# An order of work changed: VectorE's taps in the block ahead, and one block's expert layer behind the last scores

## What is computed

```python
def tok(x):                                     # 4 images, c = 64
    y = relu(bn(einsum('oc,bchw->bohw', conv1_w, x) + conv1_b))          # 16 channels
    wdyn = einsum('ok,bkhw->bohw', conv2_w, y) + conv2_b                 # 9 taps a pixel
    return einsum('bckhw,bkhw->bchw', unfold3x3(x), wdyn).reshape(b, h * w, c)

def attn(x):                                    # 4096 tokens of 64
    Q, K, V = x @ Wq + bq, x @ Wk + bk, x @ Wv + bv
    return softmax(Q @ K.T / 8) @ V

def ffn(x):                                     # 32 experts, hidden 16
    idx = argmax(x @ router_w.T + router_b)
    return relu(relu(x @ W1[idx] + b1[idx]) @ W2[idx] + b2[idx])

h = tok(x)
h = h + attn(layernorm(h))
h = h + ffn(layernorm(h))
```

## Time and profile before

| | before |
|---|---|
| median of 3 runs | 1206.12 us (1203.44 to 1207.32) |
| the profiled execution | 1203.22 us |
| its span | 1201.3 us |
| instructions | 29556 |
| idle of VectorE ahead of the copy of z (L1037) | 80.4 us in 16 |
| HBM read and written | 41.77 MB, 4.75 MB |

### The profile page before, as it was taken

How to read it: one execution, slowest core, us unless ns; L and a number is a source line. 1 busy time by engine, 2 the same in 40 slices (tenths; PEclk the granted TensorE clock), 3 DMA queues, 4 the chain that set the end, 5 groups by cost and what they waited for, 6 DMA issues and landing times.

```text
span 1201.3 us, 29556 instructions
## 1 busy us (share of the span) xinstructions
PE 1115.2 (93%) x12890; PEld 481.3 (40%) x12890; DVE 490.8 (41%) x1102; ACT 626.6 (52%) x681; POOL 10.4 (1%) x34
## 2 busy tenths in 40 slices
PE   5878999998999999999999999999899999999974
PEld 1323644443454434343444434444344343434332
DVE  6781774518072451806336081542703030311223
ACT  1545555554656455564555556465555646455531
POOL 3000000000000000000000000000000000000000
PEclk9989999999999999999999999999999999999996
DMA  7344331203032120302112030120000000000000
GB/s 195 82 106 91 83 80 37 57 1 89 1 73 57 36 55 2 91 2 63 28 28 65 1 89 2 38 54 19 19 2 11 2 10 2 10 2 10 2 10 10
DMA packets 11892, 48.52 MB, mean 40 GB/s; under 512 B 2462, under 2 KB 2590, under 8 KB 11372
## 3 DMA queue, kind: packets, MB, share of 16 engines
q1 hardware_dynamic: 11756, 46.53, 16.4%
HBM read 41.77 MB, written 4.75 MB: 39 GB/s over the span
## 4 chain that ended last, share of the span: by engine, by line
PE 65%; DVE 23%; DVEq 5%; issue 4%; DMA 2%; ACT 1%; SPq 0%; ACTq 0%
PE z_ps L592 25%; PE scores L582 23%; DVE hres L896 5%; DVEq L821 5%; PE both L550 4%; PE both L565 4%; DVE tap_product L891 2%; PE both L445 2%; DVE tap_product L846 1%; DVE tap_product L844 1%; DVE stat L842 1%; DVE stat L848 1%; DMA filter_ring<-filters 1%; PE both L546 1%; PE both L513 1%
## 5 line engine op out<-in xcount | busy, mean ns | idle before, releaser
L751 ACT ACTIVATE probs<-scores 128x1024 f32<-128x1024 f32 x480 | 465.4, 1021 | 449.2 <-PE scores L582 449.2
L582 PE MATMUL scores<-g_t,keys_t 64*64 64x512 f32 x4096 | 508.2, 591 | 4.8 <-issue 3.3
L592 PE MATMUL z_ps<-probs,keys 64*64 64x512 f32 x4096 | 510.4, 594 | 0.0
L582 PEld LDWEIGHTS scores<-g_t,keys_t 64*64 64x64 f32 x4096 | 183.8, 134 | 270.2 <-issue 257.8
L592 PEld LDWEIGHTS z_ps<-probs,keys 64*64 64x64 f32 x4096 | 173.4, 134 | 217.0 <-issue 187.6
L972 DVE COPY o_sb<-both 128x512 f32<-128x512 f32 x15 | 10.4, 692 | 459.9 <-PE both L565 459.9
L896 DVE TENSOR_TENSOR hres<-hres,tap_product 128x504 f32<-128x504 f32 (+1 forms) x128 | 89.2, 697 | 10.8 <-issue 0.4
L891 DVE SCALAR_TENSOR_TENSOR tap_product<-filter_ring,w,xin 128x504 f32<-128x504 f32 (+1 forms) x120 | 89.0, 742 | 7.0 <-DMA filter_ring<-filters 3.1
L550 PE MATMUL both<-y_t,w 64*64 64x512 f32 x496 | 66.6, 597 | 0.0
L744 ACT ACTIVATE hidden<-both 128x1024 f32<-128x1024 f32 (+1 forms) x62 | 62.6, 1010 | 3.0 <-PE both L550 3.0
L565 PE MATMUL both<-hidden,w 64*64 64x512 f32 x480 | 60.6, 591 | 0.0
(11 more groups left out here) (129 smaller groups left out, 533.1 us busy)
## 6 DMA issues: line engine op xcount, KB each, us to landing
filter_ring<-filters SPq DMA_DIRECT2D x90, 384.0 KB, 5.2
out_dram<-out_sb SPq DMA_DIRECT2D x32, 128.0 KB, 2.4
xin<-x_dram SPq DMA_DIRECT2D x6, 528.0 KB, 7.3
hidden<-once_dram SPq DMA_DIRECT2D x1, 930.0 KB, 13.1
hidden<-once_dram SPq DMA_DIRECT2D x1, 576.0 KB, 4.9
filters<-filters_sb SPq DMA_DIRECT2D x30, 18.0 KB
xin<-x_dram SPq DMA_DIRECT2D x1, 384.0 KB, 6.4
xin<-x_dram SPq DMA_DIRECT2D x1, 368.0 KB, 7.6
```

The source lines that it names most:

```text
L582: last = T.matmul(scores[rows_of(h), c, r * 512:(r + 1) * 512], keys_t[rows_of(r), n // NQ % 2, g * 128 + 64 * h:g * 128 + 64 * h + 64], g ...
L592: last = T.matmul(z_ps[rows_of(c), h, :], keys[rows_of(h), n // NQ % 2, 2 * g + r, :], probs[rows_of(h), (2 * g + c) % RING, r * 512:(r + ...
L751: A.activation(probs[:, unit % RING, :], scores[:, c, :], ACT.Exp, scale=SCALE if n else first_scale[:, 0:1]).then_inc(probs_ready, 1)
```

## The change

The plan is written anew, and four things follow from it.

- Usual blocks (3 to 15): `fin@n-2` goes from group 2 to 1, `pz` from 3 to 2, `yt` and `lg` from 6 and 7 to 5 and 6. `sum2` of block n+4 stays in group 4, and `sum0 sum1` of block n+5 stand in group 10, behind `ot`. `cc` and `cv` of a pair go from groups 1 and 4 to 4 and 7. Blocks 1 and 2 (`early_groups`) lead over to it.
- Opening: `cc@3` and `cv@3` go from block 0 into the opening, between its power steps.
- The end: `hid0` to `hid3` and `o2` of block 14 go from block 15 into the tail, between `pz@15` and `yt@15`, in the score banks and z's bank; `fin@14` goes behind `lg@15`. Of both last `o2`, ScalarE copies the lower half and VectorE adds the upper (semaphore `lower_copied`).
- SP: the filters of pair 3 are stored before block 1's are spread; a block's spread runs one block further ahead and stands behind the store of the results.

```diff
--- before.py
+++ after.py
@@ -64,7 +64,10 @@
 
 
 NONE = ("sum", "pow", "aw")
-USUAL, FIRST_TAP, TAP_PLACES, LAST = 0, 1, 6, {"hid1": 7, "hid2": 8, "o2": 9}
+USUAL, FIRST_TAP, TAP_PLACES = 0, 1, 6
+
+AT_THE_END = {f"{name}@{BLOCKS - 2}": k for name, k in (("hid0", 7), ("hid1", 8), ("hid2", 7), ("hid3", 8), ("o2", 9))}
+AT_THE_END |= {f"{name}@{BLOCKS - 1}": k for name, k in (("hid1", 7), ("hid2", 8), ("o2", 9))}
 PLACES = 10
 CHUNK = 3
 CHUNKS = TAPS // CHUNK
@@ -79,11 +82,9 @@
 def opening_groups():
     first = "tap0 tap1 tap2 tap3 tap4 tap5"
     return {
-        -1: [*at(0, "c1 " + first), *at(1, "cc cv"),
-             *at(0, "tap6 tap7 tap8 pow0 aw pow1 pow2 pow3 pow4 pow5 xt g")],
+        -1: [*at(0, "c1 " + first), *at(1, "cc cv"), *at(0, "tap6 tap7 tap8 pow0 aw pow1 pow2"), *at(3, "cc"),
+             *at(0, "pow3 pow4 pow5"), *at(3, "cv"), *at(0, "xt g")],
         0: at(1, "sum0 sum1 sum2"),
-        1: at(3, "cc"),
-        2: at(3, "cv"),
         3: at(1, "xt"),
         4: [*at(1, "g"), *at(2, "sum0 sum1 sum2")],
         7: at(2, "xt"),
@@ -94,37 +95,45 @@
     }
 
 
-def behind(m):
-
-    return {2: at(m - 1, "fin"), 3: at(m, "pz"), 6: at(m, "yt"), 7: at(m, "lg"), 10: at(m, "ot"),
-            11: at(m, "hid0"), 12: at(m, "hid1"), 13: at(m, "hid2"), 14: at(m, "hid3"), 15: at(m, "o2")}
-
-
 def merged(*plans):
     return {g: [f for p in plans for f in p.get(g, [])] for g in range(-1, PAIRS + 1)}
 
 
-def second_groups():
-    i, j = NQ, NQ + 1
-    return merged({0: at(i, "sum0"), 1: at(j, "cv"), 2: at(i, "sum1"), 4: at(i, "sum2")}, behind(0),
-                  {8: [*at(i, "xt"), *at(j, "sum0 sum1")], 9: at(i, "g"), 12: at(j, "sum2"), 16: at(j, "xt")})
+def early_groups(n):
+
+    m, i, j = n - 1, 2 * n + 2, 2 * n + 3
+    usual = {2: at(m, "pz"), 3: at(i, "sum0 sum1"), 5: at(m, "yt"), 6: at(m, "lg"), 7: at(i, "sum2"), 8: at(m, "ot"),
+             9: at(m, "hid0"), 10: at(m, "hid1"), 11: at(i, "xt"), 12: at(i, "g"), 13: at(m, "hid2"),
+             14: at(m, "hid3"), 15: at(m, "o2")}
+    if n == 1:
+        return merged(usual, {3: at(j, "cv"), 12: at(j, "sum0 sum1 sum2"), 16: at(j, "xt")})
+    return merged({0: at(i - 1, "g"), 1: at(m - 1, "fin")}, usual,
+                  {4: at(j, "cc"), 7: at(j, "cv"), 12: at(j, "sum0 sum1")})
 
 
 def usual_groups(n):
-    i, j = n + NQ, n + NQ + 1
-    ahead = {1: at(j, "cc"), 4: at(j, "cv")} if j in PAIRED else {}
-    return merged({0: at(NQ + 1, "g")} if n == 2 else {}, ahead,
-                  {0: at(i, "sum0"), 2: at(i, "sum1"), 4: at(i, "sum2")}, behind(n - 1),
-                  {8: at(i, "xt"), 9: at(i, "g")})
+
+    m, i, j = n - 1, n + NQ, n + NQ + 1
+    pair = {4: at(j, "cc"), 7: at(j, "cv")} if j in PAIRED else {}
+    groups = merged({1: at(m - 1, "fin"), 2: at(m, "pz"), 4: at(i, "sum2"), 5: at(m, "yt"), 6: at(m, "lg")}, pair,
+                    {8: at(i, "xt"), 9: at(i, "g"), 10: [*at(m, "ot"), *at(j, "sum0 sum1")]})
+    if n < BLOCKS - 1:
+        return merged(groups, {11: at(m, "hid0"), 12: at(m, "hid1"), 13: at(m, "hid2"), 14: at(m, "hid3"),
+                               15: at(m, "o2")})
+    return groups
 
 
 def last_groups():
+
     m = BLOCKS - 1
-    return merged(behind(m), {16: at(m, "fin")})
+    return merged({2: at(m, "pz"), 3: at(m - 1, "hid0 hid1 hid2 hid3 o2"), 5: at(m, "yt"), 6: at(m, "lg"),
+                   7: at(m - 1, "fin"), 8: at(m, "ot"), 9: at(m, "hid0 hid1 hid2 hid3"), 15: at(m, "o2"),
+                   16: at(m, "fin")})
 
 
 def whole_plan():
-    return [opening_groups(), second_groups(), *(usual_groups(n) for n in range(2, BLOCKS)), last_groups()]
+    return [opening_groups(), early_groups(1), early_groups(2), *(usual_groups(n) for n in range(3, BLOCKS)),
+            last_groups()]
 
 
 def split(fill):
@@ -146,9 +155,7 @@
                         continue
                     name, i = split(fill)
                     k = FIRST_TAP + int(name[3:]) % TAP_PLACES if name.startswith("tap") else USUAL
-                    if i == BLOCKS - 1:
-
-                        k = LAST.get(name, USUAL)
+                    k = AT_THE_END.get(fill, k)
                     count[k] += 1
                     self.of[fill], self.nth[fill], self.earlier[fill] = k, count[k], held.get(k)
                     held[k] = fill
@@ -253,6 +260,7 @@
         filters_loaded = [sem(f"filters_loaded{k}") for k in range(SLOTS)]
         filters_used = [sem(f"filters_used{k}") for k in range(SLOTS)]
         xn_ready, upper_hidden = sem("xn_ready"), sem("upper_hidden")
+        lower_copied = sem("lower_copied")
         y_ready, onehot_ready = sem("y_ready"), sem("onehot_ready")
         out_stored = [sem("out_stored0"), sem("out_stored1")]
         centred_ready, power_written, power_read = sem("centred_ready"), sem("power_written"), sem("power_read")
@@ -332,25 +340,25 @@
             load_image(1, 0, TILES + 2, x_loaded[1])
             sp.dma_start(staged[:, rest_of_it:], once[:, rest_of_it:]).then_inc(once_rest_loaded, 16)
             store_filters(1)
-            spread_filters(1)
             store_filters(3)
-            spread_filters(2)
-            spread_filters(3)
+            for i in range(1, NQ):
+                spread_filters(i)
             for n in range(1, BLOCKS + 2):
                 if n % NQ == 1 and n // NQ + 2 < B:
 
                     sp.wait_ge(xn_ready, NQ * (n // NQ + 1))
                     load_image(n // NQ + 2, 0, TILES + 2, x_loaded[n // NQ % 2])
+                if n > 1:
+                    store_block(n - 2)
                 if n == 1:
                     spread_filters(NQ)
                     store_filters(NQ + 1)
                     spread_filters(NQ + 1)
-                elif n + NQ < BLOCKS:
-                    spread_filters(n + NQ)
-                if n > 1:
-                    store_block(n - 2)
+                    spread_filters(NQ + 2)
+                elif n + NQ + 1 < BLOCKS:
                     if n + NQ + 1 in PAIRED:
                         store_filters(n + NQ + 1)
+                    spread_filters(n + NQ + 1)
             for k in range(2):
                 sp.wait_ge(out_stored[k], 32 * BLOCKS // 2)
 
@@ -707,6 +715,10 @@
                 elif name == "aw":
                     act.wait_ge(a_written, 1)
                     A.copy(a_w[:, :], z_ps[:, 1, 0:128]).then_inc(a_ready, 1)
+                if name == "o2" and i >= BLOCKS - 2:
+                    k = places.of[full]
+                    act.wait_ge(filled[k], places.nth[full])
+                    A.copy(o2_sb[:, :], place[k][:, 0, :]).then_inc(lower_copied, 1)
                 if name.startswith(NONE) or not name.startswith(MINE):
                     return
                 k = places.of[full]
@@ -969,8 +981,11 @@
                     normalise(h2[:, i % 2, :, :])
                     write_normalised(y_block).then_inc(y_ready, 1)
                 elif name == "o2":
-                    V.tensor_copy(o2_sb[:, :], mine[:, 0, :])
-                    settle()
+                    if i < BLOCKS - 2:
+                        V.tensor_copy(o2_sb[:, :], mine[:, 0, :])
+                        settle()
+                    else:
+                        dve.wait_ge(lower_copied, i - (BLOCKS - 3))
                     V.tensor_tensor(o2_sb[:, :], o2_sb[:, :], mine[:, 1, :], ALU.add).then_inc(done, 1)
                 else:
                     if i > 1:
```

## The result

The changed kernel takes 1159.43 us (median of 4 runs, 1157.84 to 1160.31). The ratio to the kernel before is 0.962, 95% interval 0.9597 to 0.9644: 45 us less. The forecast was 1158.5, the range 1151 to 1171.

A forecast was written before the change was run, and what follows sets the result against it. TensorE, busy 93%, was taken as the bound, stalling for late VectorE work. Stalls and gaps 38.2 + expert layer 8.3 + tail 0.8 - opening 1.5 = 45.8 us off 1203.2 or 1206.1 gave 1158.5, range 1151 to 1171.

The forecast's parts named there:

- Fin first, taps later: Blocks' new order: TensorE's stalls at `xt` and `pz` go, worth 19.7 and 12.8 us.
- the 0.18 us added to each stall: At `xt` and `pz`: a stall costs 0.18 us more than its idle figure, which counts from a modelled end.
- The taps' filters: Even blocks: the six taps wait some 6 us for filters and end near 48 us; cost nothing.
- Block 1: Block 1, with its own order: layer norm ends about 3 us before `xt`, the stall goes; 2.1 us shorter.
- The gap at the block's head: Before a block's first value group: a 0.41 us wait for z's copy goes in 14 blocks, 5.7 us.
- the spacing forecast for the blocks: Blocks 3, 5, 7, 9, 11 about 66.4 us apart, those with a pair about 68.1, before 70.6 to 71.0.
- Expert layer and tail: Block 14's expert layer: 8.3 us off block 15, 0 added behind `pz`; rest of tail 0.8 less.
- the 0.7 and 0.1 less and the 0.85 more: Tail: `pz` not waiting for `fin` 0.7 less, ScalarE copying half of `o2` 0.1 less, `ot` waiting for `fin` 0.85 more.
- 2.4 us between cold and warm: Tail from `ot` through the hidden fills: a warm clock gives 2.4 us more, a cold one 0; 0 was taken.
- Rival B: Faster case, 1154.5 us: warm tail's 2.4 us and an opening that loses nothing; chance 0.17.
- Opening: Up to block 0's end: first taps at 36.8, block 2's near 57.1, longer idling ahead of `xt`, possible cold restart.
- I take 1.5 lost: Opening: 1.5 us lost, between -1 and +4, as a cold restart delays block 0's end by 2 to 3 us.

The follow-up runs named there:

- e_three_ahead: Changed kernel with three taps of the next block ahead instead of six, the other six behind `pz`; 1185.5 us, ratio 0.9834.
- e_expert_only: Kernel before with only the end of the change (expert layer of block 14 moved into the tail); 1195.07 us, ratio 0.9925.
- e_no_bias: Changed kernel without the bias of the second expert layer, four matmuls at the head of each `o2`; one run, 1155.0 us.
- e_fin_in_z: Changed kernel with `fin` of block 14 written to the free bank of z instead of the place `ot` needs; one run, 1161.58 us.
- e_fin_in_z_warm: e_fin_in_z plus three unread fills ahead of the last `ot`, while TensorE would idle; one run, 1158.69 us.
- e_warm_block0: e_split_spread plus unread TensorE fills ahead of `xt` of blocks 1, 2 and 3 (two, two, three); 1152.27 us, ratio 0.9544.
- e_split_spread: Changed kernel with two of three parts of block 1's filters spread before pair 3 is stored, the third after; 1155.73 us, ratio 0.9591.

## Why the prediction was right

*Fin first, taps later.* Right in mechanism and size. The stalls at `xt` and `pz` were to go and went, with the margins worked out. Blocks 3 to 11 won 29.7 us; their nine `xt` stalls (17.7 less 3.2 for blocks 1 and 2, plus 0.18 each) and the nine at `pz` come to 28.9. Nine times the 0.09 us that were really in the gap at the head (below) make it 29.7. So the 0.18 us added to each stall for the modelled ends fits. `e_three_ahead` gives the stalls back, at 23 us where 22 were forecast.

*The taps' filters.* Costed at nothing, and so it was behind block 0. In block 7, whose taps need no new pair, they start right behind `onehot`. In blocks 4, 6, 8 and 10 VectorE waited 6.6 to 7.3 us for them (27.7 us in 4, where some 6 us each had been worked out), and none of it reached TensorE. A fifth wait, 4.20 us at 36.82, lies in block 0 and belongs to the opening.

*Block 1* won 3.6 us instead of 2.1. The value group behind its `xt` stall in the kernel before ran from 153.69 to 157.04, 3.35 us instead of 1.72, at a granted clock of 0.50 between 154 and 156. That spell was not in the sum, and it is chance of the one execution: in `e_expert_only`, whose block 1 is that of the kernel before, the same stall of 1.87 us is followed by a value group of 1.72 us and block 1 lasts 69.72 us. The same window in `before` and in `e_expert_only`:

```profile
154.00:157.00 3.00, 3.00 (x16) 0.96 (x12) 2.60 (x6) 0.54 (x1) 0.00 (x0) 0.50 0.02 5
```

```profile
154.00:157.00 3.00, 2.49 (x52) 1.44 (x56) 2.70 (x7) 0.59 (x1) 0.00 (x0) 1.00 0.03 8
```

So the stall cost 1.9 us (69.72 less 67.79), near the 2.05 of the sum, and the spell 1.7 more. What holds for every execution is that the changed kernel has no such stall for a spell to follow.

*The gap at the block's head*: the term that was mis-sized. "The gap before the first value group: 14 x 0.41 = 5.7" was worth 14 x 0.09 = 1.3 us. The rows showed a score group followed 2.13 us later by a value group, and a copy of z ending just before it; that it ended there was taken for the cause. The rows held the warning: in the earlier trace rows the groups in front of the gap are drawn 2.30 us long and those behind it 1.90, though both follow each other every 1.72 us. The difference is the lag behind `o2`: the 16 matmuls of such a group start over 1.8 us with the bias and over 1.4 without it (`e_no_bias`). The same error is in the spacing forecast for the blocks, 66.4 and 68.1 us, where 66.75 and 68.47 came, and in the 0.46 us from `fin` to the first value group, where 0.77 came.

*Expert layer and tail.* 8.3 us were to leave block 15, and 8.2 did (63.80 to 55.63 in `e_expert_only`, whose `fin` stays behind the first value group). Nothing was added to the path. In the tail 1.6 us went instead of 0.8: TensorE takes 0.69 and 0.67 us for `yt` and `lg`, `ot` waits for `fin` (0.6 us by `e_fin_in_z`, where 0.85 was worked out), and the hidden layer is cold (0.50 from 1137 to 1143) as was taken; and yet the fills from 1139.21 to `o2` at 1145.35 took 6.1 us instead of 6.3. The 1.6 us are 0.6 from the copy of z to `pz`, 0.3 from `yt` to `ot`, 0.2 in the hidden fills, and 0.5 behind `fin`, where nothing was changed (two later kernels with the new end have the longer time there, 5.5 us, and the others the 4.9 of the changed one). So 1.1 us at most are the change's, against 0.8 in the sum. What makes up that 0.8 is `yt` and `lg`, as the 0.7 and 0.1 less and the 0.85 more cancel but for 0.05: they took 1.13 and 1.08 us in the kernel before (granted clock 0.50 from 1175 to 1179), so 0.85 less for the two. The tails of the executions with this same end but different fronts last 35.7 to 37.2 us, and mostly the clock is what differs: up to `o2` all their steps but the hidden fills agree to 0.01 us, and these take from 6.1 us (clock 0.70 over them on average, the changed kernel) to 7.2 us (0.59, `e_three_ahead`). With a clock of 1.00 they take 4.29 us (`e_fin_in_z_warm`), which is the 4.3 that the prediction had put on a warm tail; with 0.4 for `ot` that bears out its 2.4 us between cold and warm. Rival B, at 0.17, put its 1154.5 on these 2.4 us and on an opening that loses nothing; here the clock was 0.50 from 1137 to 1143, and the 2.4 us did not come.

*Opening.* The part that was argued from rows held: 36.82 for the first taps (36.8 was forecast), 56.82 for the next (57.1). The idle stretches were 6.89, 2.88 and 2.94 us, where about 7 and, at the third, 4.7 were expected: in this execution a cold spell came behind the second `xt` (0.50 from 78 to 80), so that TensorE reached the third later and waited less, and nothing was lost. That is luck of the execution. In seven other executions of the same opening the cold restart came where it was forecast. So "I take 1.5 lost" is wrong for the profiled execution and about right over all, as far as these few tell.

The sum against the profiled execution was right to 0.4 us because errors cancelled: 4.4 us too much for the gap, against 1.8 at the opening, 1.6 in block 1 and 0.8 in the tail too little. That they cancelled so closely is luck: the cold spell in block 1 of the kernel before and the mild opening are those of single executions. Its two large terms, the stalls and the expert layer, were right each by itself.

## What to carry to other kernels

Where one engine is the bound and another half idle, look at what lies in the helper's queue ahead of each thing that the bound engine needs next, and write down for every such thing when it is done and when it is due; a margin of 1.5 us in a block of 67 was enough here, and moving the due date (`xt` three groups later) served as well as moving the work. Before a gap between two groups is called a wait, look whether the groups around it are drawn alike; here they were not (2.30 and 1.90 us), and at most 0.09 of the 0.41 us were a wait. Where TensorE waits for another engine, an unread fill can pay: laid into waits of 2.96, 3.16 and 4.89 us in block 0 such fills brought 3.5 us by the medians (`e_warm_block0`), and into one of 2.86 us in the tail 1.5 us (`e_fin_in_z_warm`), with a granted clock of 1.00 behind the last of each where it had been 0.50.

## What the runs showed of the hardware

- TensorE's 64x64 matmuls did not all start in the kernel's order: at 989.91 of the changed kernel two products of `o2` start ahead of three matmuls of the bias that stand ahead of them. The bias, two bf16 matmuls of 512 columns in each of two of the four quarters, spread the starts of a group's 16 matmuls from 1.4 to 1.8 us, unseen in the spacing of 1.72 us, until the wait for z or `fin`; leaving it out made each block that had it 0.41 to 0.44 us shorter.
- After idle stretches of 1.9 to 3.2 us the clock fell in some executions and not in others. TensorE's granted clock fell to 0.50 right behind stretches of 1.87 us (before, block 1), 2.88 us (after, block 0) and 2.96 us (`e_split_spread`, first stall of block 0), and stayed at 1.00 behind others of 1.87 us (`e_expert_only`, the same place in block 1), 2.94 us (after, 96.88) and 3.16 us (`e_split_spread`, 72.77). Behind stalls of 4.8 to 5.1 us ahead of block 3's `xt` the restart itself was cold, in all eight executions that had one.
- Block 0's length varies by 6.5 us between eight executions of kernels whose block 0 is the same (first copy of z from 121.85 to 128.38), while in those of them with the same plan behind it (the changed kernel, `e_fin_in_z`, `e_fin_in_z_warm`) the blocks from block 4 on repeat to 0.02 us (68.45 and then 66.75 and 68.47 in turn).
